# A seven-stage image pipeline on one core: key scaling moved into the token copies, token transposes moved between the point-wise halves

## The reference

```python
x = x + mixed_1x1_conv(gn(x))        # weights mixed from 8 experts by a sparsemax gate
x = x + dw3x3_then_pw1x1(gn(x))      # batch norms, relu, two prunings by the channel's maximum
x = x + attention(gn(x))             # linear attention, below
x = x + box3x3(gn(x))                # mean over 3x3
```

```python
q, k, v = split(xt @ Wqkv + bqkv);  q -= mean(q);  k -= mean(k)
k2n = k*k / (sum_c(k*k) + 1e-7);    q2n = q*q / (sum_c(q*q) + 1e-7)
k2n = k2n / max(norm_over_tokens(k2n), 1e-12)
q2n = q2n / max(norm_over_channels(q2n), 1e-12)
out = (v + q2n @ (k2n.T @ v) / sqrt(784)) @ Wln + bln
```

## Time and profile before

| what | value |
|---|---|
| median of three runs | 1752.92 us (1752.6 to 1753.8) |
| the profiled execution: time, span | 1753.74 us, 1751.6 us |
| TensorE busy | 1616.6 us, 92% |
| VectorE busy | 1587.0 us, 91% |
| ScalarE busy | 1236.8 us, 71% |
| GpSimd busy | 420.6 us, 24% |
| a full step | 51.48 us (909.65 to 961.13) |

### The profile page before, as it was taken

The page is one execution under the profiler, slowest core; times in us unless marked ns, Lnnn a source line. Parts: engine busy times, 40 slices in busy tenths (PEclk is TensorE's granted clock), DMA queues, the critical chain, the costliest instruction groups (busy, mean ns, idle before and its releaser), DMA issues.

```text
span 1751.6 us, 25475 instructions
## 1 busy us (share of the span) xinstructions
PE 1616.6 (92%) x7742; PEld 1119.3 (64%) x7742; DVE 1587.0 (91%) x2786; ACT 1236.8 (71%) x3144; POOL 420.6 (24%) x266
## 2 busy tenths in 40 slices
PE   4679999999999999999999999999999999999984
PEld 2346666666666666666666666676666667666763
DVE  6877899999999999999999999999999999998656
ACT  2366778777777877777777777777777778766662
POOL 1110321223231132323112232212222221222213
PEclk9789999999999999999999999999999999999997
DMA  4000011100011110011111001111100111000000
GB/s 137 19 19 19 19 37 38 37 24 17 34 37 37 37 37 18 18 37 37 37 37 37 18 18 37 37 37 37 37 18 18 37 37 37 19 19 19 19 19 37
DMA packets 21055, 55.54 MB, mean 32 GB/s; under 512 B 2321, under 2 KB 3345, under 8 KB 21010
## 3 DMA queue, kind: packets, MB, share of 16 engines
q1 hardware_dynamic: 20914, 54.98, 8.9%
q10 hardware_dynamic: 96, 0.00, 0.0%
HBM read 29.29 MB, written 25.69 MB: 31 GB/s over the span
## 4 chain that ended last, share of the span: by engine, by line
PE 49%; DVE 33%; issue 9%; ACT 7%; DVEq 0%; DMA 0%; POOL 0%; ACTq 0%; POOLq 0%
PE conv_ps L443 13%; PE tile_ps L533 11%; DVE h L764 7%; PE tile_ps L575 6%; PE conv_ps L563 5%; DVE xn_parts L850 5%; DVE row_sums L816 3%; PE tile_ps L500 3%; PE tile_ps L530 3%; ACT q L1107 2%; PE tile_ps L460 2%; PE tile_ps L478 2%; PE tile_ps L497 2%; DVE x L822 2%; DVE kk L864 2%
## 5 line engine op out<-in xcount | busy, mean ns | idle before, releaser
L764 DVE SCALAR_TENSOR_TENSOR h<-xpad,dw_sb,h 128x784 f32<-128x784 f32 x512 | 502.9, 1034 | 2.3
L533 PE MATMUL tile_ps<-wqk,xn_parts 128*112 128x512 f32 x1344 | 369.3, 410 | 0.0
L1202 POOL TENSOR_SCALAR xpad<-x,gn_r,gn_s 128x784 f32<-128x784 f32 x64 | 65.3, 1029 | 934.3 <-DVE gn_s L695 934.3
L533 PEld LDWEIGHTS tile_ps<-wqk,xn_parts 128*112 128x112 f32 x1344 | 216.7, 174 | 103.4 <-issue 50.9
L965 ACT ACTIVATE junk<-x 128x784 bf16<-128x784 f32 x192 | 163.7, 855 | 80.1 <-DVE x L785 41.6
L575 PE MATMUL tile_ps<-kk,xT 112*128 112x256 f32 x896 | 200.5, 381 | 3.7 <-DVE kk L864 3.7
L1088 ACT ACTIVATE q<-tile_ps 112x256 f32<-112x256 f32 x224 | 86.1, 384 | 158.8 <-PE tile_ps L533 158.8
L575 PEld LDWEIGHTS tile_ps<-kk,xT 112*128 112x128 f32 x896 | 171.0, 191 | 35.5 <-DVE kk L864 4.8
L563 PE MATMUL conv_ps<-x,mixed 128*128 128x392 f32 (+1 forms) x512 | 176.2, 497 | 2.2 <-ACT mixed L999 1.1
L443 PE MATMUL conv_ps<-h,pw_masked 128*128 128x392 f32 x512 | 175.4, 496 | 2.0 <-issue 2.0
L443 PE MATMUL conv_ps<-qT_parts,attn_parts 128*128 128x392 f32 x768 | 154.4, 350 | 8.9 <-DVE attn_parts L843 8.9
(11 more groups left out here) (136 smaller groups left out, 2997.0 us busy)
## 6 DMA issues: line engine op xcount, KB each, us to landing
x<-x SPq DMA_DIRECT2D x32, 784.0 KB, 4.3
out<-x SPq DMA_DIRECT2D x32, 784.0 KB, 3.5
expert_sb<-expert_rows SPq DMA_DIRECT2D x8, 256.0 KB, 5.2
x<-w_qk SPq DMA_DIRECT2D x1, 512.0 KB
x<-w_vT SPq DMA_DIRECT2D x1, 256.0 KB
x<-w_ln SPq DMA_DIRECT2D x1, 256.0 KB
pw_sb<-pw_wT SPq DMA_DIRECT2D x1, 256.0 KB
gmean<-group_mean SPq DMA_DIRECT2D x1, 64.0 KB, 3.9
```

What stands on the lines that cost most here:

```text
L533: mm = nc.tensor.matmul(bank, xn2_parts[:, u, i, m * TOK:(m + 1) * TOK], wqk[:, v, i, :], start=False, stop=(i == J - 1 and u == 1))
L764: ins = nc.vector.scalar_tensor_tensor(acc, view, scalar, acc, ALU.mult, ALU.add)
```

## The change

The keys are no longer scaled on VectorE. The reciprocal of a token's key sum is multiplied into the token's row of `xT` while ScalarE copies it out of PSUM (seven copies of one tile with a scale, where there were four copies, three of two tiles). `key_sums` uses the reciprocal, and its square for the fourth powers, as the stationary operand in place of ones: 14 products of 256 columns instead of seven of 512. The fourth powers are taken of the unscaled squares and after the query norms. The token transposes leave the place around `attention_out` and go between the two point-wise halves (three groups) and behind them (the fourth). `value_out` of half 1 and the gate's logits move behind the query transposes and the attention weights. VectorE's and ScalarE's orders around the queries follow, and the PSUM banks are dealt anew.

```diff
-        kk = sb("kk", [TOK, M, 2, C])
-        k2, k4 = kk[:, :, 0, :], kk[:, :, 1, :]
+        k2 = sb("k2", [TOK, M, C])
+        k4 = sb("k4", [TOK, M, C])
...
             def key_sums(D):
-                pe.wait_ge(kn_ready.sem, kn_ready.at(D))
+                pe.wait_ge(rec_step.sem, rec_step.at(D))
                 pe.wait_ge(k4_ready.sem, k4_ready.at(D))
-                for m in range(M):
-                    strip = m % STRIPS
-                    mm = nc.tensor.matmul(tile_ps[strip * SUB:(strip + 1) * SUB, KSUM_BANK, :], ones[0:TOK, 0:SUB],
-                                          kk[:, m, :, :].rearrange("p a c -> p (a c)"), start=(m < STRIPS),
+                pe.wait_ge(xT_ready.sem, xT_ready.at(D))
+                for n in range(2 * M):
+                    m, strip = n % M, n % STRIPS
+                    weight, keys, cols = (qk_rec[:, 1, m:m + 1], k2, slice(0, C)) if n < M else (k_rec2[:, m:m + 1], k4, slice(C, 2 * C))
+                    mm = nc.tensor.matmul(tile_ps[strip * SUB:(strip + 1) * SUB, KSUM_BANK, cols],
+                                          weight.to_broadcast([TOK, SUB]), keys[:, m, :], start=(m < STRIPS),
                                           stop=(m + STRIPS >= M), skip_group_check=True)
...
             def queries_keys(D):
-                before = [[(D - 1, attn_lo, J)], [(D, xT_ready, 3)], [(D, xT_ready, 4)]
+                before = [[(D - 1, qT_lo, 3)], [(D - 1, qT_lo, 4)], [(D - 1, attn_lo, J)]
                           ] + [[(D, k2_ready, m - 2)] for m in range(3, M)]
...
-            def x2_to_tokens(D, E, banks):
+            def x2_to_tokens(D, banks):
-                before = [[(E, qT_lo, 3)], [(E, qT_lo, 4)], [(D, xT_ready, 1)], [(D, xT_ready, 2)]]
+                before = [[(D, k2_ready, 5)], [(D, k2_ready, 6)], [(D, k2_ready, 7)], [(D, xT_ready, 2)]]
...
             def keys_x(D):
-                pe.wait_ge(kn_ready.sem, kn_ready.at(D))
+                pe.wait_ge(k2_ready.sem, k2_ready.at(D))
...
          @block.tensor
...
                     value_out(B, D, E, F, 0)
                     key_norms(E)
+                    q_to_channels(E, range(2))
+                    attention_weights(E)
+                    q_to_channels(E, range(2, 4))
                     value_out(B, D, E, F, 1)
-                    q_to_channels(E, range(2))
                     gate_logits(A)
-                    attention_weights(E)
-                    q_to_channels(E, range(2, 4))
-                    x2_to_tokens(D, E, range(2))
                     attention_out(E, 0)
-                    x2_to_tokens(D, E, range(2, 3))
                     attention_out(E, 1)
-                    x2_to_tokens(D, E, range(3, 4))
                     mix_experts(A)
                     queries_keys(D)
-                    pointwise(C_)
+                    pointwise(C_, range(1))
+                    x2_to_tokens(D, range(3))
+                    pointwise(C_, range(1, 2))
+                    x2_to_tokens(D, range(3, 4))
                     mixed_conv(A)
...
             def reciprocal_sums(D):
-                nc.vector.tensor_scalar(qk_rec[:], qk_sum[:], DIV_EPS, None, ALU.add).then_inc(rec_step.sem, 1)
+                nc.vector.tensor_scalar(qk_eps[:], qk_sum[:], DIV_EPS, None, ALU.add).then_inc(rec_step.sem, 1)
                 dve.wait_ge(rec_step.sem, rec_step.at(D, 1))
-                nc.vector.reciprocal(qk_rec[:], qk_rec[:]).then_inc(rec_step.sem, 1)
-            def scale_keys(D):
-                for m in range(M):
-                    nc.vector.tensor_scalar(k2[:, m, :], k2[:, m, :], qk_rec[:, 1, m:m + 1], None,
-                                            ALU.mult).then_inc(kn_ready.sem, 1)
+                if (D - 1).active:
+                    dve.wait_ge(ksum_mm.sem, ksum_mm.at(D - 1))
+                nc.vector.reciprocal(qk_rec[:], qk_eps[:]).then_inc(rec_step.sem, 1)
+                dve.wait_ge(rec_step.sem, rec_step.at(D, 2))
+                nc.vector.tensor_tensor(k_rec2[:], qk_rec[:, 1, :], qk_rec[:, 1, :], ALU.mult).then_inc(rec_step.sem, 1)
...
          @block.vector
...
-                    depthwise(B, slice(0, 2))
                     key_norms(E)
                     q_low(E, range(2))
-                    depthwise(B, slice(2, 3))
+                    depthwise(B, slice(0, 1))
+                    attention_weights_low(E)
                     q_low(E, range(2, 4))
-                    attention_weights_low(E)
+                    depthwise(B, slice(1, 3))
                     sparsemax(A)
...
-            def copy_tokens(D, banks):
+            def copy_tokens(D, tiles):
                 if (D - 1).active:
                     act.wait_ge(kx_mm.sem, kx_mm.at(D - 1))
-                for b in banks:
-                    ms = PAIRS[b]
-                    act.wait_ge(xT_mm.sem, xT_mm.at(D, b + 1))
-                    nc.scalar.copy(xT[:, ms[0]:ms[-1] + 1, :], ...).then_inc(xT_ready.sem, 1)
+                act.wait_ge(rec_step.sem, rec_step.at(D, 2))
+                for m in tiles:
+                    act.wait_ge(xT_mm.sem, xT_mm.at(D, m // 2 + 1))
+                    nc.scalar.activation(xT[:, m, :], tile_ps[0:TOK, XT_BANK[m // 2], m % 2 * C:(m % 2 + 1) * C],
+                                         ACT.Identity, scale=qk_rec[:, 1, m:m + 1]).then_inc(xT_ready.sem, 1)
...
          @block.scalar
...
                     kx_high(E)
-                    normalise_x2(A, D)
                     key_norms(E)
                     q_high(E, range(2))
+                    normalise_x2(A, D)
+                    attention_weights_high(E)
+                    q_high(E, range(2, 4))
                     x2_high(D)
-                    q_high(E, range(2, 4))
-                    attention_weights_high(E)
-                    copy_tokens(D, range(2))
                     normalise_x3(A, F)
-                    copy_tokens(D, range(2, 3))
                     relu_h(C_, 1)
-                    copy_tokens(D, range(3, 4))
...
                     relu_y(C_, 0)
-                    fourth_powers(D)
+                    copy_tokens(D, range(6))
                     relu_y(C_, 1)
+                    copy_tokens(D, range(6, M))
                     q_norms(D)
+                    fourth_powers(D)
...
-QT_BANK, KSUM_BANK, ATTN_BANK = [0, 1, 0, 1], 1, 2
-XT_BANK, QK_BANK, KX_BANK = [0, 1, 0, 1], [(m + 2) % 3 for m in range(M)], 2
+QT_BANK, KSUM_BANK, ATTN_BANK = [0, 2, 0, 2], 2, 1
+XT_BANK, QK_BANK, KX_BANK = [2, 1, 0, 2], [0, 2, 1, 0, 2, 1, 0], 1
```

More of the change, by code:

```diff
@@ L200, in build @@
         qk_sum = sb("qk_sum", [TOK, 2, M])
+        qk_eps = sb("qk_eps", [TOK, 2, M])
         qk_rec = sb("qk_rec", [TOK, 2, M])
+        k_rec2 = sb("k_rec2", [TOK, M])
         q_nsq = sb("q_nsq", [TOK, M])
@@ L258, in build @@
         k2_ready = sig("k2_ready", M)
-        rec_step = sig("rec_step", 2)
-        kn_ready = sig("kn_ready", M)
+        rec_step = sig("rec_step", 3)
         q4_ready = sig("q4_ready", M)
@@ L266, in build @@
         xT_mm = sig("xT_mm", 4)
-        xT_ready = sig("xT_ready", 4)
+        xT_ready = sig("xT_ready", M)
         kx_mm = sig("kx_mm")
@@ L513, in attention_out, with pointwise @@
                 conv_tile(j, by_parts(attn_parts, qT_parts), first=False).then_inc(attn_mm.sem, 1)
-            def pointwise(C_):
+            def pointwise(C_, halves):
                 pe.wait_ge(h_ready.sem, h_ready.at(C_))
                 pe.wait_ge(pw_masked_ready.sem, pw_masked_ready.at(C_))
-                for j in range(J):
+                for j in halves:
                     wait_free((C_ - 2, x3_ready, j + 1), (C_ + 1, x1_ready, j + 1))
@@ L607, in step @@
                 if C_.active:
-                    pointwise(C_)
+                    pointwise(C_, range(1))
+                if D.active:
+                    x2_to_tokens(D, range(3))
+                if C_.active:
+                    pointwise(C_, range(1, 2))
+                if D.active:
+                    x2_to_tokens(D, range(3, 4))
                 if A.active:
@@ L890, in step @@
                     gate_logits(A)
-                if B.active:
-                    depthwise(B, slice(0, 2))
                 if E.active:
@@ L896, in step @@
                 if B.active:
-                    depthwise(B, slice(2, 3))
+                    depthwise(B, slice(0, 1))
                 if E.active:
+                    attention_weights_low(E)
                     q_low(E, range(2, 4))
-                    attention_weights_low(E)
+                if B.active:
+                    depthwise(B, slice(1, 3))
                 if A.active:
@@ L920, in step @@
                     reciprocal_sums(D)
-                    scale_keys(D)
                 if B.active:
@@ L1046, in fourth_powers @@
             def fourth_powers(D):
-                act.wait_ge(kn_ready.sem, kn_ready.at(D))
-                nc.scalar.activation(k4, k2, ACT.Square).then_inc(k4_ready.sem, 1)
```

(4 more changed lines are left out.)

15 lines of the change are left out of this document (2 added, 13 removed).

## The result

The changed kernel takes 1742.65 us, the median of five runs (1740.99 to 1750.89), beside 1752.6 for the kernel before (five runs, 1750.94 to 1753.8). The ratio is 0.9953, 95% interval 0.9933 to 0.9972: faster by half a per cent, where the forecast was 1846.5 with a range from 1750.

A forecast was written before the change was run, and what follows sets the result against it. Two equally long chains, TensorE's product queue and VectorE's path through sparsemax and `x2_low`, were taken to bound it: 1752.9 + 27 x (2.5 collisions + 1.3 clock) - 9 = 1846.5 us. Range 1750 to 1868; the forecast's own 1800 to 1870.

The forecast's parts named there:

- `x3pad` at 44.9: ScalarE's normalised x3 ready 44.9 us after the first queries product, so box sums begin 0.85 us behind sparsemax's start.
- the token copies no longer stand in front of it: On ScalarE, the token copies were said to be gone from in front of `x3pad`, ready at 44.9 us.
- less than 2.6 us: Box sums' hold on VectorE's chain below which the change gains; 2.8 today, 5.1 forecast.
- The second: Rival: small instructions slip past, box sums hold only `mix_w` and `x2_low`; 0.6 us more a step, 1760; chance 0.11.
- The gain: Third rival: VectorE goes first and GpSimd waits, a step of 49.4 us, 1690 in all; chance 0.19.
- group means: On TensorE, 33.5 us behind the first queries product, 31.93 before plus 1.6 for the moved token transposes.
- sparsemax: On VectorE, begins 44.1 us after the first queries product.
- Key scaling: Removing 1.93 us of VectorE scalings is worth nothing while TensorE's queue is later; full price 46 us if VectorE led.
- 9 us gained: Outside the 27 steps, in step 4 and three of the drain, the second value half fills a wait: at most 4 x 2.27.
- I take 1.3: Clock loss in us a step behind TensorE's 4.5 us wait for the expert mix; bounds nothing and 1.79.
- 1860: Total time in us if, by the skill's clock rule, each of the 27 steps paid the 1.79.
- the forecast's count: Each of four box sums holds one VectorE instruction: comparison or product behind it, product for tau, gate, `mix_w`.

The follow-up runs named there:

- e11: Changed kernel with `xn2_parts` in two buffers, so `x2_high` does not wait for the second value half: 1951.43 us, ratio 1.1135.
- e2: Changed kernel with GpSimd's box sums waiting until `x2_low` is done: 1688.29 us, ratio 0.9645.
- e1: Changed kernel with ScalarE's normalise of x3 ahead of `x2_high`: 2020.14 us, ratio 1.1548.
- e7: Changed kernel with each token transpose issued twice: 1791.62 us, ratio 1.0202.
- e4: Changed kernel with seven key scalings on VectorE again, as extra work into a tile nobody reads: 1749.21 us, ratio 0.9966.
- e10: Changed kernel with box sums waiting for `x2_low` and seven key scalings back on VectorE as extra work: 1746.09 us, ratio 0.9982.
- e5: Changed kernel with 16 unused transposes in front of the expert mix in step 3 alone: 1742.01 us, ratio 0.994.
- e12: Changed kernel with 16 unused transposes in front of the expert mix in every step that has queries: 1743.3 us, ratio 0.9951.
- e3: Kernel before with GpSimd's box sums waiting until `x2_low` is done: 1760.21 us, ratio 1.0037.
- e9: Kernel before with only the new orders around the query transposes, and box sums waiting for `x2_low`: 1730.4 us, ratio 0.9873.
- e6: Changed kernel with box sums waiting for `x2_low` and 16 unused transposes before step 3's expert mix: 1685.73 us, ratio 0.9619.
- e8: Kernel before with only the new orders around the query transposes; key scaling, token transposes and copies as before: 1724.7 us, ratio 0.9832.

## Why the prediction was wrong, step by step

**The step that failed** is "`x3pad` at 44.9". ScalarE's part of the sum, "0.86 + 0.87 + 1.61 + 1.99 less 0.2 of overlaps", has no wait in it, and "the token copies no longer stand in front of it" was taken for the whole story. But `x2_high` overwrites `xn2_parts`, which the second value half still reads, and the change had moved that half behind the query transposes. The diff shows the move and the kernel shows the wait; the forecast followed what the moved products cost on TensorE and not who waits for them. It put this wait at nothing without a reason. Measured: 1.28 us of waiting, `x3pad` at 978.62, 45.9 from the first queries product of the step before (983.71 less a step of 51.02). That is 1.0 us later than forecast, while sparsemax began at 43.65, 0.45 earlier. With the box sums 2.36 instead of 0.85 us behind sparsemax's start the small instructions had time to pass. e11 takes this wait away, brings the forecast's step about in every item up to `x2_low`'s end, and turns a gain of 10 us into a loss of nearly 200. The cause is shown.

**With the hold as measured, the forecast's own sums come close, in part by luck.** It said that the change gains when the box sums hold the chain for less than 2.6 us, which makes 1752.9 - 9 = 1743.9, and that the time is about 1749 at 2.8. Measured: a hold of 2.59 (1.28 - 0.22 and 3.38 - 1.85) and 1742.65 us. With no hold it gave steps of 49.4 and 1690; e2 has 49.1 and 1688.29. But two errors of the sum stand against each other. The full steps are 0.3 us shorter than it had them, since sparsemax begins earlier: some 8 us. Step 3, at which it put nothing, took back 4.0 us in e2's trace and 14.6 in the changed kernel's (the run of 1750.89 us).

The rivals were not right either. The second (1760) has the right two instructions held, but by small ones slipping past the box sums; e1 and e11 show that small ones are held, and here they had begun before GpSimd did, except the reduction L741. It also took the second and third box sum, where the first and second did it, and its queries start at 52.0 was 1.0 us late. The gain was foreseen with 0.19, for VectorE going first with nothing held; it came with a hold of 2.59.

**Right terms**, from the changed kernel's step: group means at 33.47 (33.5), the end of the attention weights at 39.4 (39.6), sparsemax at 43.65 (44.1), VectorE waiting 1.25 us for the group means (about 1), key sums at no cost (1.85 us from 1015.33 to 1017.18, 1.84 before), transposes at 1.5 us for the 1.6 (e7). Key scaling "worth nothing as long as TensorE's queue is the later one, their full price if VectorE led": both halves are shown, by e4 (0.07 us a step) and e10 (1.8). Outside the 27 steps "9 us gained": without step 3 it is 1.9 before it, 1.7 in step 4 and 5.3 at the end, 8.9. The forecast had all of it in step 4 and the drain, where it is 7.0, so this match is partly luck.

**The clock's cost was undersized**, "I take 1.3" and bounds of nothing and 1.79 a step. In e11 the wait of 4.73 us is near the 4.5 forecast. Every step then pays about 1.5 us in the expert mix alone (3.45 instead of 1.92 in the step shown), so that its short steps are the forecast's 55.2; but eight of the 27 pay 11.8 us more, because all their queries run at half clock, which the bounds left out. In sum that is 95 us. In the changed kernel's profiled run the same cost 10.6 us in step 3. That run's granted clock over the span is 0.968 and that of the other four runs 0.973 to 0.976, which fits with its being the slowest; the four have no trace. The row on which the bounds stood was a stretch in which the clock came back. The Trainium skill's rule that a loop whose waits let the clock fall pays in every pass (TensorE: Matmul & The Clock Gate, HAM oscillation) holds in e11 for the short part and for the long part in one step of three; its figure in the forecast, 1860, was low as well.

**The rule on VectorE and GpSimd.** The Trainium skill (SBUF — State Buffer, Who interferes with whom) separates what was lumped together here: products of two SBUF inputs are held, a `tensor_scalar` can be, a reduction never is. The runs agree: beside a box sum L724 (e1) and L741 (changed kernel), both reductions, took 0.22 and 0.16 us, and the mask's reduction 1.77, as in e1 with GpSimd idle (1.78); L728 and L735 with two inputs 1.34 and 1.30, and `tensor_scalar` was held at 8, 64 and 784 columns (1.48 to 1.93). With one instruction held in each of four turns, the forecast's count came out right.

**Where the expected gain went.** 1.9 us of VectorE's work and 2.3 us of the queue in front of the attention weights were taken away; the transposes gave 1.5 back to TensorE's queue, and the box sums still hold `x2_low` for as long as before. VectorE waits 1.2 us for TensorE, TensorE 2.0 us for VectorE, and TensorE's gap closed only where GpSimd started later (e2).

**What stays open.** Why the clock stays low through the queries in some steps and not in others: every second in e1, every third in e11, and step 3 in three of seven traces behind the same wait of 4.51 us. Why the changed kernel has a tile at half clock in two of its 27 steps. And the rest of the spread of the changed kernel's runs, which neither e5 nor e12 removed.

## What to carry to other kernels

When an edit moves an operation back in a queue, list every buffer that it reads and who waits to overwrite it: the moved reader's release can set the start of something three hand-overs away. Where VectorE and GpSimd share a critical stretch, cost a schedule by how many instructions are caught, not by how large they are, and try first to put GpSimd's block behind the chain that others wait for; here it paid 1.9 us a step where VectorE had time to spare and lost some 6 to 7 us where it had none (e3, e9). An edit that relieves one queue can be worth nothing until the bound on another is gone: the key scaling was worth 0.07 us a step with the box sums early and 1.8 with them late. So try each edit beside the removal of the other's bound. And look at every step of a loop's start by itself: in the profiled executions step 3 alone moved the time by 14.6 us, more than the whole change did.

## What was new about the hardware

In step 3 of the changed kernel TensorE stayed at 1.2 GHz through 26.00 us in which it was busy for 26.00 (granted clock 0.50), and was at 1.00 in the point-wise products behind them. It is not so each time: behind the same wait of 4.51 us the clock was back within the first tile of queries in e2. In e1 the queries behind a wait of 5.17 us ran at half clock in every second step, in e11 behind 4.7 us in about every third. One such stretch costs 10.6 to 12 us. A half-clock stretch can also be short and lie within busy time: one tile of queries, 3.4 us, in two steps of the changed kernel, at a cost of 1.5 us each. Sixteen transposes in front of the mix had the clock up before it in all three traces that have them (e5, e6, e12); the fourteen token transposes of the kernel before had it in two of four (before and e8, not e3 and e9).

VectorE's smallest instructions wait for a box sum of GpSimd as the large ones do: eight columns took 1.34 to 1.89 us (e1, e11) instead of 0.17 to 0.23.
